# Two PSUM banks for the projection tiles, and batch 1's layer-norm rows built by VectorE in an attention block kernel

## The reference, cut to what matters

```python
mod = jax.nn.swish(c) @ w_mod + b_mod
sh_msa, sc_msa, g_msa, sh_mlp, sc_mlp, g_mlp = jnp.split(mod, 6, axis=1)
xn = _ln(x) * (1 + sc_msa[:, None, :]) + sh_msa[:, None, :]
q, k, v = heads_of(xn @ w_qkv + b_qkv)          # (b, head, token, 36)
q, k = _ln(q, g_q), _ln(k, g_k)
attn = jax.nn.softmax(jnp.einsum('bhqd,bhkd->bhqk', q, k) * HD ** (-0.5), axis=-1)
o = jnp.einsum('bhqk,bhkd->bhqd', attn, v)
x = x + g_msa[:, None, :] * (merge(o) @ w_proj + b_proj)
xn2 = _ln(x) * (1 + sc_mlp[:, None, :]) + sh_mlp[:, None, :]
x = x + g_mlp[:, None, :] * (jax.nn.gelu(xn2 @ w1 + b1, approximate=True) @ w2 + b2)
```

## Time and profile before

| | |
|---|---|
| median of 3 runs | 2789.83 us (2789.67 to 2790.92) |
| the profiled execution | 2789.6 us, span 2787.8 us |
| TensorE busy | 2746.5 us, 99% |
| VectorE, ScalarE, GpSimd busy | 1988.6, 1515.8, 670.7 us |
| attention, first scores to end | about 98 to 1820 us |

### The profile page before, as it was taken

How to read it: one execution, slowest core, us unless ns; L and a number is a source line. 1 busy time by engine, 2 the same in 40 slices (tenths; PEclk the granted TensorE clock), 3 DMA queues, 4 the chain that set the end, 5 groups by cost and what they waited for, 6 DMA issues and landing times.

```text
span 2787.8 us, 42816 instructions
## 1 busy us (share of the span) xinstructions
PE 2746.5 (99%) x14754; PEld 1414.7 (51%) x14754; DVE 1988.6 (71%) x2701; ACT 1515.8 (54%) x2232; POOL 670.7 (24%) x526
## 2 busy tenths in 40 slices
PE   6999999999999999999999999999999999999999
PEld 3444444444444444444444434447566575756656
DVE  7799998888888888888898899953534344353521
ACT  4777777788877777777777777631111112021110
POOL 2552343323233333333343331200000000000000
PEclk9999999999999999999999999999999999999999
DMA  6512322322211122222223243041120202112000
GB/s 223 96 34 68 91 74 79 77 50 49 54 30 32 34 66 66 70 68 72 72 73 77 57 120 112 12 158 41 51 69 24 89 6 88 41 52 69 23 18 18
DMA packets 238754, 181.28 MB, mean 65 GB/s; under 512 B 151528, under 2 KB 188078, under 8 KB 237910
## 3 DMA queue, kind: packets, MB, share of 16 engines
q1 hardware_dynamic: 238326, 179.31, 23.6%
q10 hardware_dynamic: 288, 0.04, 0.0%
HBM read 99.70 MB, written 46.04 MB: 52 GB/s over the span
## 4 chain that ended last, share of the span: by engine, by line
PE 93%; DVE 3%; ACT 1%; issue 1%; SPq 1%; POOL 1%; DMA 1%; ACTq 0%; DVEq 0%
PE at_ps L1776 18%; PE at_ps L1109 15%; PE at_ps L1106 15%; PE at_ps L1097 15%; PE at_ps L1802 15%; PE at_ps L1128 10%; DVE at_plo L890 2%; PE at_ps L1161 1%; PE at_ps L1795 1%; PE at_ps L1738 1%; PE at_ps L1755 1%; PE at_ps L1830 0%; ACT at_p L697 0%; DMA st_wm_first<-in_L_cond_b_mod 0%; PE at_ps L1139 0%
## 5 line engine op out<-in xcount | busy, mean ns | idle before, releaser
L890 DVE TENSOR_TENSOR at_plo<-at_p 128x1024 fp32r<-128x1024 f32 x1024 | 1266.7, 1258 | 184.9 <-ACT at_p L697 182.1
L697 ACT ACTIVATE at_p<-at_ps 128x1024 f32<-128x1024 f32 x1024 | 1047.0, 1025 | 407.4 <-PE at_ps L1097 406.6
L1109 PE MATMUL at_ps<-at_plo,at_vr 128*37 128x512 f32 x2048 | 1073.2, 592 | 0.0
L1106 PE MATMUL at_ps<-at_p,at_v 128*73 128x512 bf16 x2048 | 797.1, 389 | 4.9 <-DVE at_plo L890 4.7
L1776 PE MATMUL at_ps<-ml_w2s,ml_hid 128*128 128x288 f16 x3348 | 414.9, 286 | 0.0
L1802 PE MATMUL at_ps<-ml_xhi,ml_w 128*128 128x512 f16 x1296 | 381.9, 379 | 0.0
L1776 PEld LDWEIGHTS at_ps<-ml_w2s,ml_hid 128*128 128x128 f16 x3348 | 327.5, 98 | 82.0
L1106 PEld LDWEIGHTS at_ps<-at_p,at_v 128*73 128x73 f16 x2048 | 232.8, 114 | 249.3 <-DVE at_plo L890 10.5
L568 POOL TENSOR_TENSOR at_tssq<-at_tssq,head_eps 128x8 f32<-128x8 f32 x112 | 124.7, 1113 | 959.9 <-DVE at_tssq L850 959.9
L1109 PEld LDWEIGHTS at_ps<-at_plo,at_vr 128*37 128x37 f32 x2048 | 233.7, 114 | 221.5 <-issue 0.5
L1097 PE MATMUL at_ps<-at_qk_even 109*128 (+1 forms) x1024 | 309.5, 384 | 3.2 <-ACT at_p L697 3.2
(11 more groups left out here) (186 smaller groups left out, 2305.5 us busy)
## 6 DMA issues: line engine op xcount, KB each, us to landing
head_sums<-at_oT SPq DMA_DIRECT2D x256, 72.0 KB
ml_held<-head_sums SPq DMA_DIRECT2D x64, 256.0 KB
at_xy<-in_L_cond_w SPq DMA_DIRECT2D x34, 288.0 KB
w_halves<-at_wq SPq DMA_DIRECT2D x68, 144.0 KB
at_xy<-in_x SPq DMA_DIRECT2D x32, 288.0 KB, 2.9
ml_x<-in_x SPq DMA_DIRECT2D x8, 1152.0 KB, 5.5
out<-ml_x SPq DMA_DIRECT2D x7, 1152.0 KB, 4.5
ml_held<-head_rden SPq DMA_DIRECT2D x24, 216.0 KB
```

The lines of the kernel that those rows point to most:

```text
L697: act.activation(p[:, s % NP, :], ps[:, 2 * (s % 2):2 * (s % 2) + 2, :].rearrange("p a n -> p (a n)"), ACT.Exp).then_inc(exp_done, 1)
L890: nc.vector.tensor_tensor(plo[:, s % NP, :], p[:, s % NP, :], high, ALU.subtract).then_inc(plo_ready, 1)
L1106: nc.tensor.matmul(acc[0:VW, bass.ds((U % 2) * CH, CH)], v16[:, h % 2, 2 * s + a, 0:VW], high, start=(s == 0 and a == 0), stop=False, skip ...
L1109: last = nc.tensor.matmul(acc[0:RW, bass.ds((U % 2) * CH, CH)], vr[:, h % 2, 2 * s + a, 0:RW], plo[:, s % NP, a * CH:(a + 1) * CH], start= ...
```

## The change

It consists of these parts.

- **Banks.** `tile_bank` becomes a pair of banks used in turn. A tile's products wait for the scaling of the tile before the previous one. In a unit `tile_normal` moves from step 6 to step 0 of the next unit, `tile_high` to steps 1 and 2, `tile_low` to step 2, squaring and `tile_sum` to step 4.
- **Eps.** VectorE adds eps behind `tile_sum`; GpSimd keeps the power alone.
- **Rows.** Normalising in group 1, the store and load of `y_dram`, TensorE's transposes, and ScalarE's and VectorE's work on their output are gone. In groups 2 and 3 VectorE forms a row tile with tokens on partitions: `hat_scaled`, `hat_shifted` (two scalar_tensor_tensor over 576 columns against rows of scale and shift that are loaded once to all partitions), ScalarE cuts the high part (`hat_high`), VectorE the low part (`hat_lower`), and SyncE turns both with two transposing transfers into `xhi` and `xlo`. Two row tiles take three units: ten in group 2, units 1 to 15, six in group 3, units 1 to 9. The halves and the scale rows lie in parts of `qkT` that are free at the time.
- **Start.** The last chunk is four parts of one tile; `head_of` moves ahead; the first word loads go behind the first tile's transfer; VectorE's load of the branch flag goes ahead of the last part.
- **End of attention.** The reciprocal of batch 0's sums moves from unit 15 to unit 14 of group 6. In group 7 GpSimd's additions wait for the unit's first `sums`, and the multiplications move from step 3 to step 5.

```diff
-        PARTS = (..., (3, 0, 2, 7, 4), (3, 2, 3, 8, 5), (3, 3, 4, 9, 5))
+        HAT_GROUPS, HAT_FIRST, HAT_TRIPLES, HAT_SPLIT = (HATS_IN, HATS_IN + 1), (0, 6, 10), (5, 3), 3
+        PARTS = (..., (3, 0, 1, 7, 4), (3, 1, 2, 8, 4), (3, 2, 3, 9, 5), (3, 3, 4, 10, 5))
-        tile_bank, second_bank = ps[:, 7, :], ps[:, 5, :]
+        tile_pair = ps[:, 6:8, :].rearrange("p a n -> p (a n)")
+        def tile_bank(X, c0, c1):
+            return tile_pair[:, bass.ds((X % 2) * CH + c0, c1 - c0)]
...
# SyncE
-            start.load_words(sp, 0)
+            def load_hat(r):
+                sp.wait_ge(n_lo, r + 1)
+                sp.dma_start(xy[:, 0:H], xf[N + r * P:N + r * P + P, :]).then_inc(n_loaded, 16)
                     sp.dma_start_transpose(qkT[(G + 1) % 2][:, :, bass.ds(u * P, P)], ...).then_inc(t_stored, 16)
+                if U == 0:
+                    start.load_words(sp, 0)
                 if U:
                     store_sums((U - 1) // UNITS, (U - 1) % UNITS)
...
+                if r is not None:
+                    sp.wait_ge(n_lo, r + 2)
+                    if r + 1 not in (HAT_FIRST[2], NT):
+                        load_hat(r + 1)
+                    for part, whole in ((hat_hi, xhi), (hat_lo, xlo)):
+                        sp.dma_start_transpose(whole[:, :, r * P:(r + 1) * P], part[hat_in(G, u)[2]]).then_inc(n_turned, 16)
# GpSimd, tile_power
-                pool.wait_ge(t_ssq, X + 1)
-                pool.tensor_tensor(tssq[:, 1, :], tssq[:, 0, :], keep.head_eps[:, 0:QK], ALU.add).then_inc(t_msq, 1)
# ScalarE
+            def hat_high(n, r):
+                act.wait_ge(n_hat, r + 1)
+                act.wait_ge(n_turned, 32 * r + 32)
+                act.copy(hat_hi[n][:, 0:H], xy[:, 0:H])
+                act.copy(hat_hi[n][:, H:KC * P], xy[:, KF * P:H]).then_inc(n_hi, 1)
...
+                        if phase == 0 and s == 5:
+                            hat_high(area, r)
+                        if phase == 2 and s == 3:
+                            hat_high(area, r + 1)
# VectorE
+                dve.wait_ge(t_ssq, X + 1)
+                nc.vector.tensor_scalar_add(tssq[:, 1, :], tssq[:, 0, :], HD * EPS * WS * WS).then_inc(t_msq, 1)
+            def hat_scaled(n, r):
+                dve.wait_ge(n_loaded, 16 * (NT + r + 1))
+                nc.vector.scalar_tensor_tensor(out=halved(xy[:, 0:H]), in0=halved(xy[:, 0:H]), scalar=nmv[:, r, 0:1], in1=scale_row[n],
+                                               op0=ALU.subtract, op1=ALU.mult).then_inc(n_scaled, 1)
+            def hat_shifted(n, r):
+                dve.wait_ge(n_scaled, r + 1)
+                nc.vector.scalar_tensor_tensor(out=halved(xy[:, 0:H]), in0=halved(xy[:, 0:H]), scalar=nrstd[:, 1, r:r + 1], in1=shift_row[n],
+                                               op0=ALU.mult, op1=ALU.add).then_inc(n_hat, 1)
+            def hat_lower(n, r):
+                dve.wait_ge(n_hi, r + 1)
+                nc.vector.tensor_tensor(hat_lo[n][:, 0:H], xy[:, 0:H], hat_hi[n][:, 0:H], ALU.subtract).then_inc(n_lo, 1)
-                    if tail and s == (2 if first else 1):
+                    if tail and s == 0:
+                        tile_normal(U)
+                    if tail and s == 2:
                         tile_low(U)
-                    if fresh and s == 3:
+                    if fresh and s == 4:
                         tile_sum(X)
+                        phase, r, area = hat_in(G, u)
+                        # phase 0: s 1 hat_scaled(r), s 3 hat_shifted(r)
+                        # phase 1: s 1 hat_lower(r), s 6 hat_scaled(r + 1)
+                        # phase 2: s 1 hat_shifted(r + 1), s 5 hat_lower(r + 1)
# TensorE
-                    if bank is tile_bank:
-                        pe.wait_ge(t_yn, X + 1)
+                    if not isinstance(X, int) or X >= 2:
+                        pe.wait_ge(t_yn, X)
                     if G == NG:
-                        pe.wait_ge(n_lo, t + 2)
+                        pe.wait_ge(n_turned, 32 * t + 64)
-                    if G == HATS_IN and s == 4:
-                        hat_turns(u, range(KF))
-                    if G == HATS_IN and s == 7:
-                        hat_turns(u, (KF,))
# group 7, GpSimd and VectorE
+            pool.wait_ge(self.ends.pv_done, (self.UNITS_DONE - UNITS + u) * STEPS + 2)
-        if u in self.MULTIPLY_IN and s == 3:
+        if u in self.MULTIPLY_IN and s == 5:
```

215 lines of the change are left out of this document (116 added, 99 removed).

## The result

The changed kernel takes **2776.14 us** (median of 6 runs, 2774.18 to 2777.37) against 2790.15 us for the kernel before on the same chip (6 runs, 2789.67 to 2791.04). The ratio is 0.9948, 95% interval 0.9936 to 0.9961: faster by 14 us. The profiled execution took 2776.7 us with a span of 2774.8. The forecast was 2773.0, with a range of 2768.4 to 2780.0.

What follows compares the result with a forecast made beforehand. TensorE, busy 99% of the span, was taken as the bound. Terms of -2.3, -1.9, -13.07 + 1.5, -0.5 and 0 sum to -16.3 us from 2789.6: 2773.3, predicted 2773 us, range 2768.4 to 2780.0.

Steps and rivals of the forecast that it cites:

- unit 0 and the start: Start of attention: smaller parts and work moved away gain at most 1.9 us, lose up to 1; taken 0.5 gain.
- group 0, units 1 to 15: 2.3 of the 2.64 us excess goes, through two banks and word loads behind the first tile's transfer.
- groups 2 and 3: Group 2's 13.07 us excess goes; VectorE's lateness with the rows costs 1.5 us, bounds 0 and 11.
- group 7: Additions held back to step 3, multiplication at step 5; bounds -1.5 and +1.5 us, taken 0.
- the floor: Group 4's length, 215.46 us or 13.466 us per unit, with TensorE busy throughout; 17.95 us lie over it without unit 0.
- The signs of being wrong: Groups 2 and 3 or head units: `sums` wait for `plo` over 2 us; boundaries wait for last transfer; unit 0 over 14.
- The split of group 2: Group 2's 13.07 us excess: 8.5 us for TensorE's transposes, 4.6 us for tile products waiting on VectorE's scaling.
- rival B: Bank waits only handed on, VectorE's total work stops the sums, only transposes gain; 2784.5 us, chance 0.06.
- the reciprocal moves to a unit whose VectorE has 2.5 us to spare: no term: End of attention: moving the reciprocal was claimed to cost nothing, as VectorE has 2.5 us to spare there.
- The meeting that was to be pulled apart: Group 7: a second meeting of adding and GpSimd's head preparation, one unit after the first addition, pulled apart by one addition.
- Rival A: Groups 2 and 3: VectorE sets the pace, costing 11 us instead of 1.5; 2782.5 us, chance 0.13.
- Rival C: SyncE's single queue: a row tile's turn holds up the query tile, 1.37 us per row unit; 2806 us, chance 0.04.

Runs made afterwards that it cites:

- one_bank_eps: Changed kernel with one PSUM bank from the second tile on, the tile's old steps, and eps added on GpSimd again; 2791.05 us, ratio 1.0002.
- before_again: The unchanged kernel before, run once more for a second look at its start; 2791.14 us in one execution.
- rows_empty: Changed kernel with VectorE's three row instructions on 2 or 4 columns instead of 576, so rows are not normalised; 2772.35 us, ratio 0.9936.
- early_load: Changed kernel with the reciprocal in unit 13 of group 6 and phase 1 row loads issued ahead of the query tile's transfer and stores; 2774.24 us.
- late_shift: early_load with phase 0's second row instruction moved from step 3 to 5 and ScalarE's cut from step 5 to 6; 2773.18 us, ratio 0.9937.
- inv13: Changed kernel with the reciprocal moved from step 5 of unit 14 to step 5 of unit 13 of group 6; 2773.25 us, ratio 0.9942.
- g7_old: Changed kernel with group 7's addition no longer held back and the multiplication at step 3 again; 2777.34 us, ratio 0.9954.
- rows_triple: Changed kernel with the third VectorE instruction of each row tile issued three times instead of once; 2789.98 us, ratio 0.9995.

## Why the prediction was right

**The sum, by its terms** (forecast, then length of the changed kernel's profile against that of before):

| term | forecast | measured |
|---|---|---|
| unit 0 and the start | -0.5 | +0.9 (about -1.0 by medians of 11 and 3 executions) |
| group 0, units 1 to 15 | -2.3 | -1.5 |
| group 1 | -1.9 | -1.8 |
| groups 2 and 3 | -11.6 | -10.8 |
| group 6 | 0 | +1.5 |
| group 7 | 0 | -1.3 |
| sum | -16.3 | -13.0 |

The total came nearer than the terms: groups 6 and 7, both taken as nothing, are off by 1.5 and -1.3 us and cancel, which is luck.

**The main mechanism** held: lengths over the floor, and not busy shares, told what could be won. The waits of the tile products are gone, register-chosen banks cost nothing (groups 4 and 5), and groups 1 to 3 end within 1.6 us of the floor. But in groups 0 and 1 the prediction gave nearly all of the gain to the second bank, and the runs do not bear that out. one_bank_eps, without it, has group 1 at 216.39 us, 1.3 of the 1.8 us won, presumably since VectorE's old row work has left the group; and its group 0 (203.53) is at the length of before_again (203.36). Bank and eps pay there only together.

**The signs of being wrong** that the prediction named came up in part. Unit 0 took 14.86 us and not under 14. In groups 2 and 3 TensorE's matmuls stood 0.4 us for `plo`, but its weight loads 3.0, over the 2 us named. At one group boundary, that of group 7, a weight load waited 0.3 us for the last transfer. Group 2 (217.03) is just past its 217, and units 4, 11, 12 and 15 of group 0 and 0 and 4 of group 1 take 13.64 to 13.77 us, not 13.46 to 13.5.

**Groups 2 and 3.** I took 1.5 us for VectorE's lateness; it is 2.35 over the floor, 0.8 more than forecast, and 2.2 to 3.5 in the five profiles with the same row code. The places were the ones named: phase 0 in a unit with a head preparation (unit 7, and 8 behind it), and the row load that lands after step 6 (unit 12). rows_empty removes it all; early_load takes away the load's part, and late_shift, on top of it, most of the other.

**The split of group 2** in the prediction, 8.5 us for transposes and 4.6 for bank waits, was worked out as if they added up. They don't. In groups 2 and 3 the second bank is worth 2.9 us with eps on VectorE and 14.1 with eps on GpSimd. Take the rows alone (one_bank_eps) and group 2 gains 4.9 and group 3 loses 9.0; add the second bank and both come near the floor. The transposes were not taken out by themselves. What I called rival B, VectorE stopping TensorE so that only part is won, is what the row part is without the second bank.

**The step that was mis-sized** is "the reciprocal moves to a unit whose VectorE has 2.5 us to spare: no term". It measured +1.5 us. I had looked at the unit it moves to, and not at the next one: work at step 5 is done at the boundary, and the scaling, moved to step 0 of the next unit, comes late behind it; ScalarE's cut and the exponentials wait, and that last unit has no tile products to cover it. inv13 wins it back. Group 7 was left at nothing with 1.5 us on either side and came out 1.3 us shorter: 0.70 from holding the additions back (g7_old), 0.65 in unit 0, where the old place of the reciprocal is the likely cause. The meeting that was to be pulled apart was only moved, from unit 5 to unit 6.

**The start.** The bound of 1.9 us gained to 1 us lost held for the profile (+0.9), but that profile's number is chance: the clock's lower stretch and the start's shift from one execution to the next are of that size, and the forecast, which saw the lower clock, had no term for either. **Group 0** won 0.8 us less than forecast; units 4, 11, 12 and 15 keep 0.2 to 0.3 us each, and 1.3 us of its purse were chance, as before_again shows.

**Rival A** (VectorE sets the pace) did not come about, but rows_triple shows it near: each microsecond more of row work costs over half a microsecond. By the Trainium skill (SBUF — State Buffer, SBUF: two separate sides) a VectorE instruction with two inputs in SBUF and a GpSimd instruction that reads SBUF need one pair of ports under an exclusive lock, and the one that starts second blocks for the other's whole instruction. The additions of 1.11 us agree, and the one of 4.06 us shows that the loser can stay out over four instructions in a row. **Rival C** (SyncE's queue) did not come about: no wait for the query tile's transfer appears in the waits view of groups 2 and 3.

## What to carry to other kernels

Cut the span at marks that repeat, find the floor of a unit, and price a change by what lies over it; a few tenths per unit are readable when the run times are not. First see how far the same length repeats: here to 0.02 us where every engine had time to spare, and to 1.3 us in a group in which VectorE was busy 93% of the time. When work moves to a step, ask when its engine gets to that step and what covered the unit behind it. Parts of a change that free the same wait are not a sum: test each without the other before crediting it.
